# The last layer of a Perceiver-like kernel: half of the experts' outputs weighed on ScalarE and summed on GpSimd, the result stored by tiles

## The reference

```
x = hidden_states.reshape(-1, H)                        # 2048 tokens x 256
probs = softmax(x @ router_w.T)                         # 8 experts
top_w, top_i = top_k(probs, 2);  top_w /= sum(top_w)
combine = sum(top_w[..., None] * one_hot(top_i, 8), axis=1)
def bitlinear(x, w):                                    # x to 8 bits by its row's maximum, w to -1/0/1
    return x_q @ w_q.T
def expert_ffn(x, gw, uw, dw):
    return bitlinear(bitlinear(x, uw) * square(relu(bitlinear(x, gw))), dw)
for e in range(8):
    out = out + combine[:, e:e+1] * expert_ffn(x, gate_w[e], up_w[e], down_w[e])
result = x_before + out
```

## Time and profile before

| | |
|---|---|
| median of 3 runs | 2399.45 us (2393.07 to 2401.55) |
| the profiled execution's own time | 2394.15 us |
| its span in the trace | 2392.3 us, 49762 instructions |
| busy over the whole span | PE 1949.1 us (81%), PEld 1405.8 (59%), DVE 1855.7 (78%), ACT 1387.5 (58%), POOL 566.4 (24%) |
| sixth layer, first up group to last `output` | about 1989 to 2385 us from the span's start |
| busy in 1989 to 2385 (396 us) | PE 263.39, PEld 145.71, DVE 362.31, ACT 313.81, POOL 43.22 |

### The profile page before, as it was taken

The page is one execution under the profiler, slowest core; times in us unless marked ns, Lnnn a source line. Parts: engine busy times, 40 slices in busy tenths (PEclk is TensorE's granted clock), DMA queues, the critical chain, the costliest instruction groups (busy, mean ns, idle before and its releaser), DMA issues.

```text
span 2392.3 us, 49762 instructions
## 1 busy us (share of the span) xinstructions
PE 1949.1 (81%) x15356; PEld 1405.8 (59%) x15356; DVE 1855.7 (78%) x5143; ACT 1387.5 (58%) x3645; POOL 566.4 (24%) x721
## 2 busy tenths in 40 slices
PE   6999999999998775666899999999868766666665
PEld 6877777777775553333677777677656643333333
DVE  4588888888887466995787887877457787999997
ACT  1255566566553444443466666666545556788876
POOL 0022222222221000110333433433134441010100
PEclk9999999999999997777899999999966777898888
DMA  2011111111110102001012211211010000000000
GB/s 93 10 31 30 30 30 30 30 28 28 29 30 28 65 1 98 1 1 40 24 54 64 60 54 53 67 28 31 19 28 11 11 10 2 0 0 0 0 0 36
DMA packets 63869, 70.78 MB, mean 30 GB/s; under 512 B 40034, under 2 KB 41380, under 8 KB 62756
## 3 DMA queue, kind: packets, MB, share of 16 engines
q1 hardware_dynamic: 63780, 69.76, 10.1%
HBM read 63.02 MB, written 2.10 MB: 27 GB/s over the span
## 4 chain that ended last, share of the span: by engine, by line
PE 49%; DVE 30%; issue 10%; ACT 8%; DVEq 1%; POOL 1%; DMA 0%; ACTq 0%; SPq 0%; POOLq 0%
PE ps L625 4%; PE ps L647 3%; DVE f_act L2543 3%; PE ps L634 3%; DVE f_ams L2559 3%; PE ps L1863 3%; PE ps L663 3%; PE ps L1803 3%; PE ps L693 3%; PE ps L596 2%; PE ps L1793 2%; PE ps L1846 2%; PE ps L1872 2%; ACT a_pr L377 2%; PE ps L2226 2%
## 5 line engine op out<-in xcount | busy, mean ns | idle before, releaser
L377 ACT ACTIVATE a_pr<-ps,a_nm 128x257 f32<-128x257 f32 x512 | 238.1, 473 | 172.8 <-DVE a_nm L492 172.8
L1595 ACT ACTIVATE d_pr<-d_st,d_nm 128x257 f32<-128x257 f32 x256 | 128.2, 502 | 191.0 <-DVE d_nm L1715 177.3
L500 DVE COPY a_pT<-ps 128x512 f32<-128x512 f32 x256 | 170.1, 685 | 60.1 <-PE ps L663 59.6
L492 DVE TENSOR_REDUCE a_nm<-ps 128x2 f32<-128x514 f32 x256 | 174.5, 682 | 0.0
L663 PE MATMUL ps<-ident,a_pr 128*128 128x128 f32 x1024 | 159.0, 278 | 0.0
L2633 PE MATMUL ps<-f_wt,f_nxT 128*128 128x512 bf16 x512 | 145.8, 436 | 8.9 <-DVE f_act L2543 8.4
L313 POOL TENSOR_TENSOR a_sf<-a_sf,a_ratio 128x256 f32<-128x256 f32 x64 | 39.4, 615 | 473.2 <-DVE a_ratio L521 473.2
L2657 PE MATMUL ps<-f_wt,f_nhT 128*128 128x256 bf16 x512 | 76.8, 300 | 87.0 <-ACT f_nhT L2473 87.0
L1846 PE MATMUL ps<-d_kc,d_qc 128*128 128x257 f32 x512 | 142.1, 401 | 0.0
L663 PEld LDWEIGHTS ps<-ident,a_pr 128*128 128x128 f32 x1024 | 120.6, 144 | 25.7 <-issue 12.7
L625 PE MATMUL ps<-a_cT,a_wqk 128*128 128x257 f32 x512 | 132.8, 381 | 2.9 <-DVE a_k L465 1.7
(11 more groups left out here) (351 smaller groups left out, 5306.6 us busy)
## 6 DMA issues: line engine op xcount, KB each, us to landing
a_cT<-in_ctx SPq DMA_DIRECT2D x64, 257.0 KB, 2.7
d_cT<-in_ctx SPq DMA_DIRECT2D x64, 257.0 KB, 2.8
f_wf<-in_f_w SPq DMA_DIRECT2D x24, 512.0 KB, 3.8
a_vbd<-a_vself SPq DMA_DIRECT2D x256, 8.0 KB
e_vb<-e_vs SPq DMA_DIRECT2D x256, 8.5 KB
c_wf<-in_c_w SPq DMA_DIRECT2D x3, 1024.0 KB, 7.2
x_all<-in_x SPq DMA_DIRECT2D x1, 2048.0 KB, 7.8
d_wo<-in_d_wo SPq DMA_DIRECT2D x1, 2048.0 KB
```

What stands on the lines that cost most here:

```text
L377: ins = act.activation(pr[j][:, g, :], ps[:, S_BANK[u % 2] + k, S:LK], ACT.Exp, bias=nm[j][:, g:g + 1], accum_out=ssum[j][:, 0, g:g + 1])
L492: dve.tensor_reduce(nm[j][:, 2 * u:2 * u + 2], ps[:, s0:s0 + 2, S:LK], AX.X, ALU.max, negate=True).then_inc(max_ready.sem, 1)
L500: dve.tensor_copy(pT[u][:, :, :, :], ps[:, T_BANK[u % 2], :].rearrange("p (g c q) -> p g c q", g=2, c=2))\
L1595: ins = act.activation(pr[j][:, g, :], st[u][:, k, :], ACT.Exp, bias=nm[u][:, k:k + 1], accum_out=sm[j][:, g:g + 1])
```

## The change

In the sixth layer only the first expert's output of a pair is still weighed and added to `x` on DVE. The second expert's output is weighed by ACT: one ACTIVATE (`weighed`, Copy with the weight as per-partition scale) reads the second half of bank 7 and writes it to SBUF, to `f_acc` for pair 0 and to one of three tiles `f_yw` for the others. GpSimd sums: `add` adds a `f_yw` to `f_acc`, three times a tile, and `add_to_tile` adds `f_acc` to `x` when DVE has added its four. That last sum counts `tile_done`; `finish_tile` is gone from this layer. SP stores every tile by a DMA of its own when it is counted. Every tile's output is the same sum as before in another order.

```
     def sp(eng):
         ...
+        for t in range(NT):
+            layer_wait(eng, n + 1, t + 1)
+            eng.dma_start(out[:, t, :], x_all[:, t, :]).then_inc(out_stored.sem, 16)
     def pool(eng):
...
-            for t in range(NT):
-                normed_input(t)
-                rounded_input(t, t % 2)
+            def add(t, u):
+                eng.wait_ge(w_out.sem, w_out.at(t, u + 1))
+                if u > 1:
+                    eng.wait_ge(acc_done.sem, acc_done.at(t, u - 1))
+                eng.tensor_tensor(acc[t % 2][:, :], acc[t % 2][:, :], yw[u - 1][:, :], ALU.add).then_inc(acc_done.sem, 1)
+            def add_to_tile(t):
+                eng.wait_ge(y_out.sem, y_out.at(t + 1, 0))
+                eng.wait_ge(acc_done.sem, acc_done.at(t + 1, 0))
+                eng.tensor_tensor(x_all[:, t, :], x_all[:, t, :], acc[t % 2][:, :], ALU.add).then_inc(tile_done.sem, 1)
+            ...
+            for t in range(NT + 1):
+                if t > 0:
+                    add(t - 1, 1)
+                if t + 1 < NT:
+                    rounded_input(t + 1, (t + 1) % 2)
+                if t > 0:
+                    add(t - 1, 2)
+                    add(t - 1, 3)
+                    add_to_tile(t - 1)
+                if t + 2 < NT:
+                    normed_input(t + 2)
     # scalar
+                def weighed(u):
+                    ...
+                    act.wait_ge(y_out.sem, y_out.at(t, u + 1))
+                    if pair:
+                        if not first:
+                            act.wait_ge(acc_done.sem, acc_done.at(tile - 1, pair))
+                    elif not first:
+                        layer_wait(act, n + 1, tile - 1)
+                    to = yw[pair - 1] if pair else acc[parity]
+                    act.activation(to[:, :], ps[:, 7, HID:2 * HID], ACT.Copy, scale=ams[pair][:, 4, 1:2])\
+                        .then_inc(w_out.sem, 1)
-                for u in range(PAIRS if more else PAIRS + LAG):
+                for u in range(PAIRS if more else PAIRS + LAG + 1):
                     gate(u, 0)
                     gate(u, 1)
-                    turned_out(u - LAG)
+                    weighed(u - LAG - 1)
+                    if u - LAG < PAIRS:
+                        turned_out(u - LAG)
     # vector, sizes(u)
+                    if not first:
+                        dve.wait_ge(w_out.sem, w_out.at(t - 1, u + 1))
     # vector, output(u)
-                    for k in range(2):
-                        dve.wait_ge(y_out.sem, y_out.at(t, 2 * u + k))
-                        dve.scalar_tensor_tensor(x, ps[:, 7, k * HID:k * HID + HID], ams[u % PAIRS][:, 4, k:k + 1], x,
-                                                 ALU.mult, ALU.add).then_inc(y_out.sem, 1)
-                    if u == -1:
-                        dve.wait_ge(y_out.sem, y_out.at(t, 0))
-                        finish_tile(dve, n + 1, t - 1)
+                    dve.wait_ge(y_out.sem, y_out.at(t, u))
+                    dve.scalar_tensor_tensor(x, ps[:, 7, 0:HID], ams[u % PAIRS][:, 4, 0:1], x, ALU.mult, ALU.add)\
+                        .then_inc(y_out.sem, 1)
     # tensor, down(u)
-                    pe.wait_ge(y_out.sem, y_out.at(t, 2 * u))
+                    pe.wait_ge(y_out.sem, y_out.at(t, u))
+                    pe.wait_ge(w_out.sem, w_out.at(t, u))
     # sync, at the end of the program
-        enter(sp, len(phases))
-        sp.dma_start(y_view, x_all[:, :, :]).then_inc(out_stored.sem, 16)
-        sp.wait_ge(out_stored.sem, out_stored.at(1, 0))
+        sp.wait_ge(out_stored.sem, out_stored.at(NT, 0))
```

More of the change, by code:

```diff
@@ L122, in build @@
     tile_done = signal("tile_done")
+    out_stored = signal("out_stored", 16)
     aggr_ready, var_ready = signal("aggr_ready", NT), signal("var_ready")
@@ L1078, in ternary_ffn @@
             shared("both_up_psum_t_done", 2, NT), shared("both_sil_done_exp_in", 2, NT), shared("both_h_ready_exp_done", 2, NT),
-            shared("both_ms_done_dif_done", 1, NT), shared("both_h3_ready_xb_done", 1, NT),
+            shared("both_ms_done_dif_done_w_out", 1, NT), shared("both_h3_ready_xb_done", 1, NT),
             shared("both_hs_done_kn_ready_kf_ready", 1, NT))
-        nh_ready, nhT_psum, nhT_ready, y_psum = (shared("both_nh_ready_ln_in", 1, NT), shared("both_nhT_psum_ln_done", 1, NT),
+        nh_ready, nhT_psum, nhT_ready, y_psum = (shared("both_nh_ready_ln_in_acc_done", 1, NT), shared("both_nhT_psum_ln_done", 1, NT),
                                                  shared("both_nhT_ready_sc_ready", 1, NT), shared("y_psum", 1, NT))
@@ L1976, in gated_attention @@
                                     shared("both_h_ready_exp_done", 2, NT))
-        dif_done, u_done = shared("both_ms_done_dif_done", 1, NT), shared("both_hs_in_u_done_nxf_ready", 1, NT)
+        dif_done, u_done = shared("both_ms_done_dif_done_w_out", 1, NT), shared("both_hs_in_u_done_nxf_ready", 1, NT)
         kn_ready, z_half, z_ready = (shared("both_hs_done_kn_ready_kf_ready", 1, NT), shared("both_scaled_exp_done_z_half", 1, NT),
                                      shared("both_ra_ready_p_ready_z_ready", 1, NT))
-        ln_in, ln_done = shared("both_nh_ready_ln_in", 1, NT), shared("both_nhT_psum_ln_done", 1, NT)
+        ln_in, ln_done = shared("both_nh_ready_ln_in_acc_done", 1, NT), shared("both_nhT_psum_ln_done", 1, NT)
         pT_psum, pT_ready, o_psum = shared("pT_psum", 1, NT), shared("pT_ready", 1, NT), shared("o_psum", 1, NT)
@@ L2359, in experts @@
         nhT = [sb(f"f_nhT{j}", [P, 2, IK, P], BF16) for j in range(2)]
+        acc = [sb(f"f_acc{j}", [P, HID]) for j in range(2)]
+        yw = [sb(f"f_yw{j}", [P, HID]) for j in range(NE // 2 - 1)]
         wr_loaded = signal("f_wr_loaded", 32)
@@ L2374, in experts @@
                                                      signal("f_hT_ready", PAIRS), shared("y_psum", PAIRS, NT),
-                                                     signal("f_y_out", NE))
+                                                     signal("f_y_out", PAIRS))
+        w_out, acc_done = shared("both_ms_done_dif_done_w_out", PAIRS, NT), shared("both_nh_ready_ln_in_acc_done", PAIRS - 1, NT)
         EPS = 1e-5
@@ L2418, in rounded_input @@
                 plink.end()
-            for t in range(NT):
-                normed_input(t)
-                rounded_input(t, t % 2)
+            def add(t, u):
[7 more added lines that the diff above has]
+                eng.tensor_tensor(x_all[:, t, :], x_all[:, t, :], acc[t % 2][:, :], ALU.add).then_inc(tile_done.sem, 1)
+            normed_input(0)
+            rounded_input(0, 0)
+            normed_input(1)
+            for t in range(NT + 1):
[9 more added lines that the diff above has]
+                    normed_input(t + 2)
         def scalar(act):
@@ L2474, in turned_out @@
                         .then_inc(hT_ready.sem, 1)
-                for u in range(PAIRS if more else PAIRS + LAG):
+                def weighed(u):
+                    if first and u < 0:
+                        return
+                    tile, pair, parity = (t, u, s) if u >= 0 else (t - 1, u + PAIRS, 1 - s)
+                    act.wait_ge(y_out.sem, y_out.at(t, u + 1))
[8 more added lines that the diff above has]
+                for u in range(PAIRS if more else PAIRS + LAG + 1):
                     gate(u, 0)
                     gate(u, 1)
-                    turned_out(u - LAG)
+                    weighed(u - LAG - 1)
+                    if u - LAG < PAIRS:
+                        turned_out(u - LAG)
                     if u - 1 < PAIRS:
@@ L2593, in step @@
                 elink.end()
-                if not more:
-                    dve.wait_ge(y_out.sem, y_out.at(t, NE))
-                    finish_tile(dve, n + 1, t)
             parts = (rounded, router_scores, router_shares)
@@ L2678, in build @@
     block = root.enter_context(nc.Block())
-    y_view = out
-    out_stored = signal("out_stored", 16)
     def enter(eng, n):
```

## The result

The changed kernel takes 2439.01 us (2437.55 to 2445.34, 4 runs) against 2399.94 us of the kernel before, run beside it. The ratio is 1.0165, with a 95% interval from 1.0136 to 1.0194: it is slower by 39 us. 2403 us were predicted, with 2418 as the upper end.

The account below looks back on a forecast made before the run. VectorE bounded the kernel at 24.09 us a tile; afterwards the ScalarE-TensorE loop would. 340.2 + 1.35 x 16 - 355.3 + 0.4 - 2.8 gave +4 us: 2403 against the median 2399.45, range 2387 to 2418.

Parts of the forecast that it names:

- VectorE relieved to 21.67 us a tile, no longer the bound: Last layer: VectorE's tile falls from 24.09 to 21.67 us, and the bound passes to the ScalarE-TensorE loop.
- The weighing, 0.37 to 0.44 us, and its place in the loop: On ScalarE between last square and `turned_out`: taken as 0.40 us, lengthening a pair from 5.365 to 5.77 us.
- the loop: Closed chain over ScalarE and TensorE in the last layer: `turned_out`, `down`, `up`, `gate`, `turned_out`; 5.365 us a pair before.
- 1.35 us for a low-clock pair: Last layer: each pair with TensorE at 1.2 GHz costs 1.35 us more, from 6.84 against 5.41, some partly caught.
- n = 16: Pairs at TensorE's low clock among the last layer's 59: 27% taken, between 22% and half, making +4 us.
- -17.5 + 1.35 n: Change in us over the last 59 pairs, first tile and end included, with n pairs at the low clock.
- 22% and one half: Low-clock shares of TensorE's up groups before: 11 of 49 not waiting for VectorE, 5 of 10 waiting.
- The third rival: TensorE's longer pause in every pair makes the low clock common: n = 30, 2422 us, chance 0.21.
- No cost from the new waits, GpSimd and the stores: Last layer: ScalarE's and VectorE's new waits, GpSimd's sums and moved `normed_input`, and SP's fifteen 128 KB stores cost zero.
- The first tile, +0.4: Last layer's first tile runs as before, apart from one weighing on the loop: 0.4 us more.
- The end, 2.8 us less: From the last `down` to the last store's landing: 5.0 us instead of 7.8, between a loss of 1 and gain of 3.

Follow-up runs that it names:

- e9_fill3: The changed kernel with three extra matmuls of 256 columns a pair, result unused, on TensorE right after the transposes; 2410.10 us, ratio 1.0040.
- e3_copy: The kernel before with one unrelated ScalarE copy of 128x256 a pair between the gate and the copy to `f_nhT`; 2454.79 us, ratio 1.0226.
- e1_stores: The kernel before with only SP's storing of each tile when it is counted; 2396.64 us, ratio 0.9984.
- e2_no_weigh: The changed kernel without the weighing on ScalarE and its sums on GpSimd, second expert's output left out; 2385.82 us, ratio 0.9938.

## Why the prediction was wrong

- **VectorE relieved to 21.67 us a tile, no longer the bound:** right that it is no longer the bound. The weighings and the statistics took 35 us out of the 59 pairs, 2.4 a tile as reckoned; the 21.67 itself isn't seen, since VectorE now waits. Its share fell to 76 instead of 88, because the tile became longer than expected.
- **The weighing, 0.37 to 0.44 us, and its place in the loop:** right in the place, a little short in the size. The instruction lasts 0.46 us and the plain pitch rose by 0.39 (5.365 to 5.75; against the 5.32 without the weighing it is 0.43). Its group, and GpSimd's, in the changed kernel:

```profile
L2518 ACT ACTIVATE f_yw<-ps,f_ams 128x256 f32<-128x256 f32 x43 | 19.6, 456 | 0.0
...
L2432 POOL TENSOR_TENSOR f_acc<-f_acc,f_yw 128x256 f32<-128x256 f32 x48 | 34.8, 725 | 285.9 <-ACT f_yw L2518 285.9
```

- **1.35 us for a low-clock pair:** right to 0.1. It is 1.45 in the changed kernel, 1.43 in e9_fill3 ((361.2 - 339.8) / 15).
- **n = 16, "I take 27%, nearer to the first kind":** this step failed. It was 43 of 60, 72%. The formula -17.5 + 1.35 n gives +40.6 for n = 43; 39 was measured. I named n as what everything hangs on, and then held it between two shares seen in the kernel before, 22% and one half. Neither bounds it. In the kernel before the loop was held by VectorE, with another rhythm in each of a tile's four steps, and its groups don't tell what a loop does whose pause is longer in each pair. From the runs: about 6 low-clock pairs more for each 0.1 us in the loop (19, 32 and 43 for 0, 0.20 and 0.43), where I had allowed some 3 in all for 0.40. The rate is of these three kernels and no more; e3_copy has 47 at 5.69 us.
- **The third rival,** a common low clock from the longer pause: the right mechanism as far as the runs separate it, with 0.21 and with n = 30, too small.
- **No cost from the new waits, GpSimd and the stores:** right as far as the traces show. The wait of the weighing for VectorE's output occurs only at the end, TensorE never waited for `f_xn` within the 59 pairs, and the stores alone changed nothing there (e1_stores). The collision of the sums with VectorE, for which there was no row, is small: its clamp takes 0.714 us in the mean instead of 0.685, one small operation 0.209 instead of 0.169 (0.686 and 0.169 in e2_no_weigh, without the sums), some 4 us over the 59 pairs of an engine that waits.
- **The first tile, +0.4:** mis-sized, it is 1.9 us longer.
- **The end, 2.8 us less:** mis-sized, 3.7. The end before is 8.5 us and not 7.8, since the sum left out the 0.35 us of issuing the store and what follows its landing. The 128 KB landed in 1.8 instead of 2.5 us; the sums took 0.725 instead of 0.615.

What stays open: why so small a change of the pause moves the clock so much, and whether it does so by its length or because VectorE's late clamp no longer splits it. The runs show how the count goes with the loop's length and with the work in the pause; they don't show by what rule the chip decides, and I tried none.

## What to carry to other kernels

Where two engines hand work to each other in a loop, find the loop's pitch before moving work to the engine that looks idle: idle time on the far side of the hand-over doesn't cover an instruction on the near side, and against the kernel without the weighing (345.4 us) the same 0.46 us cost 57 us of the 59 pairs in the one place and 9 in the other. When TensorE is in such a loop and already drops to its low clock at times, don't price the low clock from the kernel before; try the change with extra matmuls in the pause, which here told in one run that the low clock was the cost, and was worth 63 us. An operation's own duration says little about its price: the 46 us here are 25 of weighing (59 x 0.43) and 31 for the 24 low-clock pairs more than without it, less the 11 that VectorE's relief gave back (356.3 to 345.4).

## What the runs showed of the hardware

- Extra matmuls whose result is unused made the kernel faster: eight of 256 columns a pair took the granted clock from 0.82 to 1.00 and 63 us off the time.
- One unrelated ScalarE copy of 0.40 us a pair made 59 pairs of the kernel before 45.6 us longer, 0.77 us for each, nearly twice its own duration.
- TensorE was busy 67 us of 100 in the changed kernel and ran 43 of 60 pairs at the low clock, with a mean wait of 2.23 us ahead of a down group. In the kernel before it was busy 66 of 100, with 16 such pairs and a mean wait of 1.36 us. The busy share alone doesn't tell.
